# Gated cross-attention with routed experts: a hand-set list of slots in place of three-stage turns, and the last tile through all experts

## The chip, the cores and the metric

The kernel runs on one core of a Trainium2 chip. The time is the device time in microseconds, as the median of three runs; lower is better.

## The reference

For each of 8 batches of 112 tokens (256 wide) the layer attends with 16 heads of 16 over 375 context rows (192 wide), adds the gated result to x, and sends each token to one of 8 experts with room for 112 tokens each.

```python
x = x + jnp.tanh(g_xattn[0]) * _L0_xattn_ref(_layernorm(x), ctx_768, ctx_768, Wq, bq, Wk, bk, Wv, bv, Wo, bo)
x = x + jnp.tanh(g_ffn[0]) * _L0_ffn_ref(_layernorm(x), wg, W, b)
# _L0_xattn_ref:
attn = jax.nn.softmax(jnp.einsum('bhqd,bhkd->bhqk', q, k) * SCALE, axis=-1)
out = jnp.einsum('bhqk,bhkd->bhqd', attn, v)      # heads side by side, @ Wo + bo
# _L0_ffn_ref:
idx = jnp.argmax(probs, axis=-1)
locations = jnp.cumsum(mask, axis=0) - mask       # place of a token in its expert
mask = mask * (locations < C)                     # C = 896 / 8 = 112
exp_out = jnp.einsum('ech,efh->ecf', exp_in, W) + b[:, None, :]
out = jnp.einsum('tec,ecf->tf', combine, exp_out) # combine holds the gate
```

## The kernel before, in words

**Accuracy.** Scores are made in bf16 at float32 accuracy: K and Q are each split into three bf16 parts (the high part, the rest rounded, and what then remains), and six products of parts are stacked as 96 contraction rows. DMAs lay the parts of all heads into these rows (`lay_rows`, L340, K at L347, Q at L350: six of each a batch). Three more rows hold ones under K and the negated row maxima (again in three parts) under Q, so that the turned scores come out with the maximum already taken off.

**Turns.** A step t (L353 on SyncE, L518 on TensorE, L676 on ScalarE, L843 on VectorE, L1001 on GpSimd) works on three batches at once: it projects K, Q and V of batch t, takes the plain scores and their maxima of batch t-1, and the turned scores, exponentials and probability products of batch t-2. Steps 0, 1, 8 and 9 are written out, 2 to 7 are two turns of a loop of three steps (`turns`, L285). A step has 12 units; `heads_of` (L85), `AT_K1`, `AT_V2` and their like say what a unit holds.

**TensorE in a step.** K and Q of half 0 at the start (`project_kq`, L424), a second K half (L408), Q (L418) and its bias (L421) in the units, the scores (L442) into the banks `sc0` and `sc1` by turns, four turned heads a unit (L450), the product with V (L459), and at the end V (L435) and the product with Wo (L514). `scores` of a step wait for the copies of K and Q rows (L538), the first turned unit for the row of maxima (L530).

**The others.** VectorE takes each maximum from its bank (L848), subtracts the high part (`split`, L839), splits the maxima (L878 to L882), normalises the probability product (L904 to L911) and adds x (`add_x`, L820). ScalarE copies the projections out and rounds (L637), and exponentiates (L686). GpSimd makes the third part (L1007). SyncE issues the row copies.

**Router and experts.** Tiles 0 to 6 are routed together (`route`, L766, `assign`, L791), tile 7 after its own x2; GpSimd scatters all eight tiles into slots in DRAM (L962). They are cleared first (L364), read back by expert (L381), turned and multiplied (L606), and stored by an indirect DMA for each expert (L1050).

Of the kernel before, what the change touches and what calls it, by code (L numbers as in the profile page):

```python
# [26 lines left out]
QC = NK  # L53
KQ = NK + NQ
# [4 lines left out]

TWO_ONES = float(np.array([0x3F803F80], np.uint32).view(np.float32)[0])  # L60
MAXROW = 128 - 3
FAR = 4096
RING = 3

AT_K1, AT_Q1, AT_SPLIT1 = (1, 2), (3, 4), 5
FIRST_HEADS = 1
AT_V2, AT_V2E = (6, 7), 9
AT_V_OF_1 = (2, 3, 5, 6, 8, 9)
AT_MAXT, AT_MAXT_B = 11, 10

EARLY = 5
NORMED = ((0, B - 2), (B - 2, B - 1), (B - 1, B))
ROUTED = ((0, B - 1), (B - 1, B))


AT_STAT2, AT_NORM2, AT_TURN2 = 2, (5, 6, 7), (6, 7, 8)
AT_X1, AT_NORM6, AT_TURN3, AT_ROUTE, AT_PLACES = 1, 3, (2, 3, 4, 6), 8, 9
# [4 lines left out]
THREE = 4  # L82


def heads_of(unit):  # L85

    at = 2 * (unit - FIRST_HEADS)
    return range(max(at, 0), min(at + 2, H))


def build(nc, x, ctxT, gx, gf, wq, bq, wk, wv, wo, bo, wg, wT, be, out):
    slots = nc.dram_tensor("slots", (SLOTS, ROW), F32).ap()
    out_rows = out.rearrange("b n d -> (b n) d")
    with ExitStack() as stack:
# [6 lines left out]

        wq_sb = sb("wq_sb", [128, 2, D])
        bq_sb = sb("bq_sb", [1, D])
        wk_sb = sb("wk_sb", [128, 2, D])
        wv_sb = sb("wv_sb", [128, 2, D])
        wo_sb = sb("wo_sb", [128, 2, D])
        bo_sb = sb("bo_sb", [NQ, D])
        tbo = sb("tbo", [NQ, D])
        wg_sb = sb("wg_sb", [128, 2, E])
        wT_sb = sb("wT_sb", [128, E, 2, D])  # L110
        be_sb = sb("be_sb", [NQ, E, D])
# [4 lines left out]
        ones_row = sb("ones_row", [1, NQ])  # L116
# [3 lines left out]
        expert_no = sb("expert_no", [NQ, B, E])  # L120

# [3 lines left out]
        ctx_sb = sb("ctx_sb", [128, RING, 2, NK])  # L125
# [17 lines left out]

# [4 lines left out]
        onorm = sb("onorm", [128, 2, NQ])  # L148
        st2 = sb("st2", [NQ, B, 6])
# [21 lines left out]
        xin = sb("xin", [CAP, E, ROW])  # L171

        xinT, yb, res = xnT, xn, x_sb

# [7 lines left out]

        s_x = sem("first_x_loaded")
        s_xrest = sem("x_rest_loaded")
        s_gate = sem("gates_loaded")
        s_tanh = sem("tanh_ready")
# [4 lines left out]
        s_bo = sem("bo_loaded")  # L191
# [3 lines left out]
        s_pad = sem("rows_96_on_ready")  # L195
        s_vones = sem("v_ones_ready")
        s_ctx = sem("ctx_loaded")
        s_ctx1 = sem("ctx_1_loaded")
# [5 lines left out]
        s_kq = sem("kq_in_psum")  # L204
        s_hi = sem("kq_hi_ready")
        s_rest = sem("kq_rest_ready")
        s_mid = sem("kq_mid_ready")
        s_parts = sem("kq_parts_ready")
        s_lo = sem("rest_used")
        s_first = sem("first_kq_read")  # L210
        s_k6 = sem("kq_rows_laid")
        s_k60 = sem("kq_rows_of_0_laid")
# [7 lines left out]
        s_lastrows = sem("last_max_rows_ready")  # L220
        s_identv = sem("identity_for_dve")
# [3 lines left out]
        s_pv = sem("pv_in_psum")  # L225
        s_on = sem("normalised")
        s_op = sem("wo_product_in_psum")
        s_x1 = sem("x1_ready")
        s_outx = sem("x1_in_out")
        s_xn2a = sem("xn2_of_0_to_2_ready")  # L230
        s_xn2 = sem("xn2_ready")
        s_nmean = sem("first_rstd_ready")
        s_wg = sem("wg_loaded")
        s_wT = sem("experts_loaded")
# [3 lines left out]
        s_tri = sem("triangle_ready")  # L238
        s_eno = sem("expert_numbers_ready")
# [5 lines left out]
        s_empty = sem("empty_rows_ready")  # L245
# [7 lines left out]
        s_free = sem("product_read")  # L253
        s_be = sem("expert_biases_loaded")
        s_res = sem("result_ready")
        s_out = sem("out_stored")
# [3 lines left out]
        class Seen:  # L260

            def __init__(self):
                self.n, self.base = {}, {}

            def start_turn(self):
                self.base = dict(self.n)

            def __call__(self, s, more=1):  # L270
                had = self.n.get(s.name, (s, 0))[1]
                self.n[s.name] = (s, had + more)
                return had + more

        def settle(eng, seen):


            eng.drain()
            for name, (s, n) in seen.n.items():
                before_turn = seen.base.get(name, (s, 0))[1]  # L280
                if n > before_turn:
                    eng.sem_inc(s, before_turn - n)
            seen.n = {name: seen.base.get(name, (s, 0)) for name, (s, n) in seen.n.items()}

        def turns(eng, seen, step):  # L285


            for t in range(2):
                step(t, t)
            seen.start_turn()  # L290
            with eng.Fori(0, (B - 2) // RING) as i:
                for k in range(RING):
                    step(2 + k, 2 + k + RING * i)
                settle(eng, seen)
            for t in range(B, B + 2):
                step(t, t)

        def front(t):
            return t < B

# [797 lines left out]
```

## Time and profile before

| | us |
|---|---|
| median of 3 runs | 296.07 (293.12 to 302.96) |
| profiled execution | 294.2 |
| its span, first to last instruction | 292.5 |
| TensorE busy, granted clock | 200.9 (69%), 0.819 |
| VectorE busy | 139.9 (48%) |
| ScalarE busy | 87.0 (30%) |
| GpSimd busy | 63.5 (22%) |

The profile gives busy times for each engine, and for each idle stretch what ended it. Matmuls are pipelined, so that the distance from one start to the next tells more than a duration. A float32 call of the source stands as two instructions in the trace. PE is TensorE, DVE VectorE, ACT ScalarE, POOL GpSimd, SP SyncE. The granted clock is a share of 2.4 GHz.

### The profile page before, as it was taken

What the parts mean: (1) busy time and instruction counts of PE and PEld (TensorE: products, weight loads), DVE (VectorE), ACT (ScalarE), POOL (GpSimd) and SP (SyncE); (2) the same over time, 40 slices, a digit from 0 to 9 for tenths busy, and PEclk for the clock granted to TensorE, in tenths of its full rate; (3) what the DMA queues carried; (4) which work ended last, traced back from release to release, by engine and by line L of the source; (5) the groups of instructions that cost most, each with busy time, mean ns of one, the idle gap of its engine ahead of it and who ended that gap; (6) DMA issues with size and microseconds to landing.
All of it is one profiled execution on the core that took longest, in us unless ns stands there. A gap on an engine that the chain in (4) does not pass through costs nothing. (4 is left out here: it accounts for less than half of the span.)

```text
span 292.5 us, 4359 instructions
## 1 busy us (share of the span) xinstructions
PE 200.9 (69%) x1703; PEld 126.1 (43%) x1703; DVE 139.9 (48%) x311; ACT 87.0 (30%) x180; POOL 63.5 (22%) x67
## 2 busy tenths in 40 slices
PE   2685148399569975997399659957981998712590
PEld 1463024266335643554156326633640566512370
DVE  4179948248405731573167127622850764522270
ACT  1320030136122602360245125402531365400120
POOL 4439990011010101010101011001100201073064
PEclk9979558869977987699789859975995799965597
DMA  4979459806980895079409930990399948052731
GB/s 132 228 73 98 37 60 121 69 0 65 119 64 2 83 124 43 0 88 123 37 0 97 122 26 12 108 120 6 43 99 154 321 136 237 2 158 87 221 94 53
DMA packets 36840, 26.77 MB, mean 92 GB/s; under 512 B 15528, under 2 KB 34074, under 8 KB 36714
## 3 DMA queue, kind: packets, MB, share of 16 engines
q1 hardware_dynamic: 32453, 21.40, 59.7%
q10 hardware_dynamic: 3349, 2.67, 3.5%
q0 software_dynamic: 1024, 2.51, 2.8%
q8 instruction: 9, 0.15, 0.3%
q14 instruction: 5, 0.04, 0.1%
HBM read 9.25 MB, written 5.52 MB: 51 GB/s over the span
## 5 line engine op out<-in xcount | busy, mean ns | idle before, releaser
L848 DVE TENSOR_REDUCE nmax<-sc 112x1 f32<-112x375 f32 x128 | 67.2, 546 | 58.4 <-PE sc L442 57.5
L686 ACT ACTIVATE prob<-stp 128x448 f32<-128x448 f32 (+1 forms) x80 | 43.0, 542 | 69.1 <-PE stp L450 68.2
L442 PE MATMUL sc<-k,q 125*112 125x375 bf16 x128 | 45.7, 386 | 20.9 <-DMA k<-parts 15.9
L1007 POOL TENSOR_TENSOR parts<-rest,parts 128x487 bf16<-128x487 f32 x16 | 17.1, 1071 | 157.2 <-ACT parts L637 157.0
L408 PE MATMUL pj<-ctx_sb,wk_sb 128*128 128x375 f32 x64 | 35.0, 666 | 17.8 <-DMA ctx_sb<-in_ctxT 17.1
L450 PE MATMUL stp<-q,k 128*128 128x112 bf16 (+1 forms) x320 | 33.1, 238 | 14.6 <-DMA q<-mrows 14.6
L459 PE MATMUL pv<-prob,v_sb 128*32 128x112 f32 (+1 forms) x768 | 38.5, 281 | 0.4 <-ACT prob L686 0.3
L450 PEld LDWEIGHTS stp<-q,k 128*128 128x128 bf16 (+1 forms) x320 | 22.6, 124 | 27.2 <-issue 16.9
L442 PEld LDWEIGHTS sc<-k,q 125*112 125x112 bf16 x128 | 17.8, 149 | 31.6 <-DMA k<-parts 17.1
L839 DVE TENSOR_TENSOR rest<-pj,parts 128x487 f32<-128x487 f32 x16 | 10.5, 659 | 34.0 <-ACT parts L637 34.0
L459 PEld LDWEIGHTS pv<-prob,v_sb 128*32 128x32 f32 (+1 forms) x768 | 15.8, 111 | 23.7 <-issue 14.8
L408 PEld LDWEIGHTS pj<-ctx_sb,wk_sb 128*128 128x128 f32 x64 | 15.3, 257 | 23.7 <-DMA ctx_sb<-in_ctxT 13.3
L637 ACT ACTIVATE parts<-pj 128x487 bf16<-128x487 f32 x16 | 9.2, 578 | 38.3 <-PE pj L421 38.3
L435 PE MATMUL pj<-wv_sb,ctx_sb 128*128 128x256 f32 (+1 forms) x72 | 19.1, 388 | 0.0
L763 DVE TENSOR_SCALAR xn<-x_sb,mv,rs 112x256 f32<-112x256 f32 x8 | 17.1, 2182 | 3.3 <-POOL rs L957 3.3
L637 ACT ACTIVATE parts<-rest 128x487 bf16<-128x487 f32 x16 | 9.7, 608 | 19.5 <-DVE rest L839 18.9
L418 PEld LDWEIGHTS pj<-xnT,wq_sb 128*128 128x128 f32 x64 | 12.1, 225 | 4.1 <-issue 1.9
L435 PEld LDWEIGHTS pj<-wv_sb,ctx_sb 128*128 128x128 f32 (+1 forms) x72 | 12.7, 187 | 2.0 <-issue 1.0
L418 PE MATMUL pj<-xnT,wq_sb 128*128 (+1 forms) x64 | 12.1, 303 | 0.5 <-DMA bq_sb<-in_bq 0.5
L962 POOL DMA_INDIRECT slots<-rows,slot x8 | 8.0, 1006 | 13.8 <-DVE slot L804 12.1
L435 PE MATMUL stp<-wv_sb,ctx_sb 128*128 128x256 f32 (+1 forms) x24 | 9.0, 511 | 2.1 <-DMA wv_sb<-in_wv 2.1
L1050 POOL DMA_INDIRECT out<-x_sb,xin x8 | 7.8, 972 | 12.2 <-issue 12.2
(100 smaller groups left out, 200.7 us busy)
## 6 DMA issues: line engine op xcount, KB each, us to landing
k<-parts SPq DMA_DIRECT2D x48, 187.5 KB, 7.3
q<-parts SPq DMA_DIRECT2D x48, 56.0 KB, 6.9
ctx_sb<-in_ctxT SPq DMA_DIRECT2D x8, 281.2 KB, 7.2
wT_sb<-in_wT ACTq DMA_DIRECT2D x1, 2048.0 KB, 14.7
slots<-xin SPq DMA_DIRECT2D x1, 1799.0 KB, 15.8
xin<-slots SPq DMA_DIRECT2D x8, 224.9 KB, 5.0
be_sb<-in_be SPq DMA_DIRECT2D x1, 896.0 KB, 6.1
x_sb<-in_x SPq DMA_DIRECT2D x1, 784.0 KB, 11.6
```

The costliest lines, as they stand in the source:

```text
L408: pe.matmul(pj[m][:, 0:NK], wk_sb[:, c, m * 128:(m + 1) * 128], ctx_sb[:, t % RING, c, :], start=(c == 0), stop=(c == 1))
L418: pe.matmul(pj[m][:, QC:KQ], wq_sb[:, c, cols], xnT[:, bass.ds(tb, 1), c, :], start=(c == 0), stop=False)
L435: mm = pe.matmul(bank[0:kn, at:at + D], ctx_sb[:, t % RING, c, k0:k0 + kn], wv_sb[:, c, :], start=(c == 0), stop=(c == 1))
L442: pe.matmul(sc[h % 2][0:NQ, 0:NK], q6[0:MAXROW, b3, h, :], k6[0:MAXROW, b3, h, :], start=True, stop=True).then_inc(s_sc, 1)
L450: mm = pe.matmul(bank_of_sT(t, n)[0:kn, j * NQ:(j + 1) * NQ], k6[:, b3, h, k0:k0 + kn], q6[:, b3, h, :], start=True, stop=True)
L459: mm = pe.matmul(pv[32 * j:32 * j + 32, g * NQ:(g + 1) * NQ], v_sb[0:kn, b3, c, 4 * g + j, :], prob[0:kn, n % 3, j * NQ:(j + 1) * NQ], sta ...
L637: nc.scalar.activation(dst, src, ACT.Copy).then_inc(signal, 1)
L686: nc.scalar.activation(prob[0:kn, n % 3, :], bank_of_sT(t, n)[0:kn, 0:4 * NQ], ACT.Exp, scale=SCALE).then_inc(s_p, 1)
L763: nc.vector.tensor_scalar(xn[:, b, :], x_sb[:, b, :], mv1[:, b, 0:1], rs1[:, b:b + 1], ALU.subtract, ALU.mult).then_inc(s_xn, 1)
L839: nc.vector.tensor_tensor(rest[:, m, :], pj[m][:, 0:KQ], parts[:, t % RING, 0, m, :], ALU.subtract)\
L848: nc.vector.tensor_reduce(nmax[:, h:h + 1], sc[h % 2][0:NQ, 0:NK], axis=AX.X, op=ALU.max, negate=True).then_inc(s_max, 1)
L1007: ins = nc.gpsimd.tensor_tensor(parts[:, t % RING, 2, m, :], rest[:, m, :], parts[:, t % RING, 1, m, :], ALU.subtract)
```

## The change

1. **Slots.** All engines run through one list of slots from -4 to 120, twelve a batch, without a loop. At slot s, `at(s, offset)` tells which batch and which of its twelve places stands there. A batch's scores begin at 12b, its K projection at 12b-16, its K rows are laid at 12b-7, V is projected at 12b+12 to 12b+17 (batch 0: 2 to 7), the maxima are split at 12b+13 and turned at 12b+14, turned scores begin at 12b+17, products with V a slot later, the normalisation stands at 12b+30, Wo at 12b+31, x is added at 12b+32, and the logits come at 12b+36.
2. **Q** is made for groups of 1, 4 and 3 batches, all early, and laid by 18 DMAs in place of 48. Its bias is added as ScalarE copies it out and VectorE subtracts.
3. **K's split**: ScalarE copies the projection out twice (bf16 and float32, `k_hi`, `k_copy`), and from batch 1 on GpSimd does both subtractions and the rounding (`k_split`). K's rows of a partition lie side by side, so that a copy has half as many pieces of twice the length (1500 bytes). GpSimd also splits the maxima.
4. **Context** stays whole in SBUF, loaded in four DMAs; there is no ring. The score product has 96 rows in place of 125 and needs no zeros there.
5. **Router.** Tiles 0 to 5 are routed at slots 97 to 99, tile 6 at 109 to 111, and both are scattered while attention of batch 7 still runs.
6. **Last tile.** Tile 7 is not scattered. It is multiplied by all eight experts (`dense`, 8 calls of 512 columns), and VectorE adds the eight products with a weight which is the token's gate for its expert and 0 elsewhere. The biases come by a product of the turned weights with the expert biases.

Cut to its core (the code after):

```python
HEADS = ((0, 1), (2,), (3,), (4, 5), (6,), (7,), (8, 9), (10,), (11,), (12, 13), (14,), (15,))
K_AT, KE_AT, KSPLIT_AT, LAY_AT = -16, (-14, -12), (-13, -11), -7
V01_AT, V01E_AT, V2_AT, V2E_AT, V_EARLY = 12, 16, 16, 18, -10
SPLITMAX_AT, MAXT_AT, MROW_AT, T_AT, PV_AT = 13, 14, 15, 17, 18
NORM_AT, WO_AT, ADD_AT, LN_AT, X2T_AT, LG_AT = 30, 31, 32, 33, 35, 36
QG = ((0, 1), (1, 5), (5, 8))
...
# TensorE
for s in range(FIRST, LAST + 1):
    if s == 0: turn_xn(1); project_q(1, 0); project_q(1, 1)
    if (found := at(s, T_AT)): scores_T(*found)
    if (found := at(s, S_AT)): scores(found[0], HEADS[found[1]][0])
    if (found := at(s, K_AT, 4)) and found[0] > 0: project_k(*found)
    ...
    if s == 5: turn_xn(2)
    if s in (6, 7): project_q(2, s - 6)
    ...
    if found := at(s, PV_AT): probs_v(*found)
pe.wait_ge(s_wT, 16 * E)
dense(0); dense(1); places(2, *R2); dense(2); dense(3)
...
# SyncE
def lay_k(b):
    if b >= KR: sp.wait_ge(s_st, UNITS * (b - KR + 1))
    for part, ready in ((0, s_khi), (1, s_kmid), (2, s_klo)):
        sp.wait_ge(ready, 2 * (b + 1))
        ...
# GpSimd
def k_split(b, m):
    ...
    nc.gpsimd.tensor_tensor(kf[:, b % 2, m, :], kf[:, b % 2, m, :],
                            parts_k[:, b % 2, 0, m, :], ALU.subtract).then_inc(s_krest, 1)
    pool.wait_ge(s_krest, 2 * b + m + 1)
    nc.gpsimd.tensor_copy(parts_k[:, b % 2, 1, m, :], kf[:, b % 2, m, :]).then_inc(s_kmid, 1)
    k_lo(b, m)
for s in range(FIRST, LAST + 1):
    if s == 2: q_lo(1, 0); q_lo(1, 1)
    if s == 4: rstd(2)
    if found := at(s, SPLITMAX_AT, 1): split_max(found[0])
    for m in range(2):
        if (found := at(s, KSPLIT_AT[m], 1)) and found[0] > 0: k_split(found[0], m)
    if s == 6: constants()
    if s == 9: q_lo(2, 0); q_lo(2, 1)
    ...
# VectorE, of the slots that the text speaks of
    if s == 2: statistics(5, 8)
    if s == 4: normalise(2)
# VectorE, after the slots
for e in range(E):
    link(nc.vector.scalar_tensor_tensor(last[:, :], banks[e // 2][0:NQ, (e % 2) * D:(e % 2 + 1) * D],
         share[:, e:e + 1], src, ALU.mult, ALU.add))
```

On TensorE, at the seam of two steps of the loop, before (stp is a bank of turned scores, sc one of scores, pj one of a projection, mparts the parts of the maxima):

```order
L558 MATMUL sc<-ident_b,mparts 48x112
L459 MATMUL pv<-prob,v_sb 32x112 x8
L435 MATMUL pj<-wv_sb,ctx_sb 128x256 x4
L514 MATMUL misc<-wo_sb,onorm 112x256 x2
L408 MATMUL pj<-ctx_sb,wk_sb 128x375 x2
L418 ISA
L418 MATMUL pj<-xnT,wq_sb 128x112
L418 ISA
L418 MATMUL pj<-xnT,wq_sb 128x112
L421 MATMUL pj<-ones_row,bq_sb 128x112
L450 MATMUL stp<-q,k 128x112 x8
L442 MATMUL sc<-k,q 112x375
```

And the slots 6 to 8 of a later batch now, where a batch's last product with V has just passed (L425 scores, L438 turned scores, L456 product with V, L478 Wo, L400 K):

```order
L425 MATMUL sc<-k,q 112x375 x2
L456 MATMUL pv<-prob,v_sb 32x112 x4
L438 MATMUL stp<-q,k 119x112 x4
L425 MATMUL sc<-k,q 112x375
L478 MATMUL misc<-wo_sb,onorm 112x256 x2
L456 MATMUL pv<-prob,v_sb 32x112 x4
L438 MATMUL stp<-q,k 128x112 x4
L425 MATMUL sc<-k,q 112x375
L400 MATMUL pj<-ctx_sb,wk_sb 128x375
L456 MATMUL pv<-prob,v_sb 32x112 x4
L438 MATMUL stp<-q,k 128x112 x4
L425 MATMUL sc<-k,q 112x375
```

V, Wo, K and Q stood together between two batches' turned scores, and there was no score among them; now Wo stands between a score and a product with V of the next batch, and K is spread over slots.

On SyncE's queue, in a step of the loop before (parts copied into the k and q rows, and the load of a context):

```order
L350 DMA q<-parts 16x16x112 x2
L355 ISA
L355 DMA ctx_sb<-in_ctxT 96x2x375
L350 DMA q<-parts 16x16x112
L347 DMA k<-parts 16x16x375 x2
L350 DMA q<-parts 16x16x112 x2
L347 DMA k<-parts 16x16x375 x2
L350 DMA q<-parts 16x16x112
```

Now, for a batch in the middle (L334 the row of maxima, L312 six K copies, L317 two experts' weights, whose tile shares its room with x's turned rows under the name early):

```order
L334 DMA q<-mrows 3x16x112
L312 DMA k<-parts_k 16x8x750 x6
L317 DMA early<-in_wT 128x512 x2
L334 DMA q<-mrows 3x16x112
L312 DMA k<-parts_k 16x8x750 x6
```

The Q copies and the context loads have gone from the steady part, and the row of maxima, which ScalarE's queue issued before, stands ahead of the next K copies.

On GpSimd, the end of its constants and what follows, before (L1020 adds the bias to x, L1007 is the third part):

```order
L997 IOTA expert_no 112x64
L1020 TENSOR_TENSOR x_sb<-x_sb,tbo 112x2048
L1007 TENSOR_TENSOR parts<-rest,parts 128x487 x2
L291 UNCONDITIONAL_BRANCH
L1007 TENSOR_TENSOR parts<-rest,parts 128x487 x6
```

At slot 9 GpSimd's stream has Q's last group (L977), x plus bias (L1051) and seven constants; this is the end of the constants and what follows them, up to the first half of batch 2's K and the first maxima (L967, L970 and L961 are a half's subtraction, rounding and subtraction; L985 to L988 split the first maxima):

```order
L1024 MEMSET every 112x112
L1025 MEMSET before 112x112
L1026 AFFINE_SELECT before<-before 112x112
L1029 IOTA expert_no 112x64
L967 TENSOR_TENSOR kf<-kf,parts_k 128x375
L970 CAST parts_k<-kf 128x375
L961 TENSOR_TENSOR parts_k<-kf,parts_k 128x375
L985 CAST mparts<-nmax 112x16
L986 TENSOR_TENSOR mrest<-nmax,mparts 112x16
L987 CAST mparts<-mrest 112x16
L988 TENSOR_TENSOR mparts<-mrest,mparts 112x16
```

The first maxima are behind the last Q group, the bias, the constants and one half of K's split.

## Rows read from the trace of the kernel before

**Rows 1.** The page, its part 1: busy us (share of the span), instructions
```profile
PE 200.9 (69%) x1703; PEld 126.1 (43%) x1703; DVE 139.9 (48%) x311; ACT 87.0 (30%) x180; POOL 63.5 (22%) x67
```

**Rows 2.** Table by stretch: from:to, length, engines busy (instructions), granted clock, DMA share, GB/s
```profile
0.00:41.00 41.00, 18.84 (x68) 12.25 (x68) 24.87 (x32) 8.89 (x17) 27.91 (x29) 0.82 0.68 103
91.00:101.00 10.00, 10.00 (x126) 6.07 (x124) 8.09 (x17) 6.04 (x12) 1.05 (x1) 1.00 0.44 49
102.45:131.40 28.95, 23.55 (x198) 14.22 (x199) 12.96 (x28) 9.60 (x19) 2.22 (x2) 0.82 0.62 63
241.10:254.70 13.60, 11.43 (x179) 8.19 (x179) 5.72 (x24) 7.22 (x17) 0.81 (x2) 1.00 0.46 129
254.70:292.50 37.80, 14.43 (x66) 10.86 (x66) 12.42 (x39) 3.43 (x10) 16.65 (x18) 0.68 0.40 119
```

**Rows 3.** List of waits: who <- whom, us in total, times, longest us
```profile
...
DVE nmax L848 <- PE sc L442: 57.5, 63, 7.9
...
PE sc L442 <- DMA k<-parts: 15.9, 6, 4.7
...
PE stp L450 <- DMA q<-mrows: 14.6, 6, 5.7
...
```

**Rows 4.** Timeline of TensorE, 84 to 101.5: start us, us, engine, line, operation
```profile
90.94 0.79 PE L408 MATMUL pj<-ctx_sb,wk_sb 128*128 128x375 f32 x2
91.57 0.32 PE L442 MATMUL sc<-k,q 125*112 125x375 bf16 x1
...
92.15 0.37 PE L450 MATMUL stp<-q,k 128*128 128x112 bf16 x4
92.36 0.33 PE L442 MATMUL sc<-k,q 125*112 125x375 bf16 x1
92.52 0.37 PE L418 MATMUL pj<-xnT,wq_sb 128*128 x2
...
92.98 0.40 PE L459 MATMUL pv<-prob,v_sb 119*32 119x112 f32 x8
93.32 0.37 PE L450 MATMUL stp<-q,k 128*128 128x112 bf16 x4
...
96.65 0.60 PE L435 MATMUL pj<-wv_sb,ctx_sb 128*119 128x256 f32 x2
97.08 0.32 PE L442 MATMUL sc<-k,q 125*112 125x375 bf16 x1
```

**Rows 5.** Costliest groups of the page; then the timeline of VectorE after a batch
```profile
L848 DVE TENSOR_REDUCE nmax<-sc 112x1 f32<-112x375 f32 x128 | 67.2, 546 | 58.4 <-PE sc L442 57.5
...
102.45 0.65 DVE L904 STREAM_TRANSPOSE pvT<-pv 128x448 f32<-128x448 f32 x1 [0.88 <-PE pv L459]
...
103.84 0.41 DVE L911 STREAM_TRANSPOSE onorm<-onT 128x224 f32<-128x224 f32 x1
```

**Rows 6.** Timeline, 237 to 262: the last row of maxima, its copy and use
```profile
239.91 0.26 ACT L637 ACTIVATE mrows<-sc 48x112 bf16<-48x112 f32 x1 [0.21 <-PE sc L558]
...
242.56 0.57 PE L450 MATMUL stp<-q,k 128*128 128x112 bf16 x8 [1.52 <-DMA q<-mrows]
```

**Rows 7.** Timeline of the lead-in; a costly group and a DMA group of the page
```profile
22.55 13.98 DVE L763 TENSOR_SCALAR xn<-x_sb,mv,rs 112x256 f32<-112x256 f32 x5 [1.66 <-POOL rs L957]
22.65 7.96 POOL L982 MEMSET k<- 32x3000 f32 x3
...
L1007 POOL TENSOR_TENSOR parts<-rest,parts 128x487 bf16<-128x487 f32 x16 | 17.1, 1071 | 157.2 <-ACT parts L637 157.0
...
k<-parts SPq DMA_DIRECT2D x48, 187.5 KB, 7.3
```

**Rows 8.** Timeline of GpSimd at the end: the first and the last of eight stores
```profile
278.66 0.94 POOL L1050 DMA_INDIRECT out<-x_sb,xin  x1 [9.52 <-issue]
...
288.15 0.94 POOL L1050 DMA_INDIRECT out<-x_sb,xin  x1 [0.30 <-issue]
```

More of the change, by code:

```diff
@@ L52 @@
 UNITS = G * NCH
-QC = NK
-KQ = NK + NQ
 K_PART = (0, 0, 0, 1, 1, 2)
@@ L257, in build @@
+        s_last = sem("last_tile_ready")
         s_chain = sem("vector_chain")
         s_pchain = sem("gpsimd_chain")
[L260 to L299, printed above, removed]
-        def maxima(t):
-            return 1 <= t <= B
-        def attention(t):
-            return t >= 2
@@ new lines, in _ @@
+            pe.wait_ge(s_wT, 16 * E)
+            dense(0)
+            dense(1)
+            places(2, *R2)
+            dense(2)
+            dense(3)
+            pe.wait_ge(s_share, 1)
+            pe.transpose(sc[0][0:E, 0:NQ], share[:, :], ident[0:NQ, 0:NQ]).then_inc(s_shareT, 1)
+            pe.wait_ge(s_shareTe, 1)
+            pe.wait_ge(s_be8, 16)
+            pe.matmul(pv[0:NQ, 0:D], shareT[:, :], be8[:, :], start=True, stop=True).then_inc(s_bias, 1)
+            for e in range(E):
+                turn_xin(e)
+                if e == 1:
+                    pe.wait_ge(s_last, 1)
@@ new lines, in _ @@
+            for e in range(E):
+                if e % 2 == 0:
+                    dve.wait_ge(s_dense, e // 2 + 1)
+                src = rows[:, b, X1:X1 + D] if e == 0 else last[:, :]
+                link(nc.vector.scalar_tensor_tensor(
+                    last[:, :], banks[e // 2][0:NQ, (e % 2) * D:(e % 2 + 1) * D], share[:, e:e + 1],
+                    src, ALU.mult, ALU.add))
+            dve.wait_ge(s_bias, 1)
+            nc.vector.tensor_tensor(last[:, :], pv[0:NQ, 0:D], last[:, :], ALU.add).then_inc(s_last, 1)
@@ L960, in scatter, with rstd @@
-            def scatter(lo, hi):
-                for b in range(lo, hi):
-                    nc.gpsimd.indirect_dma_start(
-                        slots, bass.IndirectOffsetOnAxis(ap=slot[:, b:b + 1], axis=0), rows[:, b, :],
-                        None, bounds_check=SLOTS - 1, oob_is_err=False).then_inc(s_scat, 16)
+            link = Chain(pool, s_pchain)
+            def rstd(g):
+                lo, hi = QG[g]
+                pool.wait_ge(s_stat, g + 1)
+                link(nc.gpsimd.tensor_scalar(ve1[:, lo:hi], mv1[:, lo:hi, 1], EPS, None, ALU.add))
+                nc.gpsimd.tensor_tensor(rs1[:, lo:hi], ve1[:, lo:hi], half[:, lo:hi], ALU.pow)\
+                    .then_inc(s_rstd, 1)
@@ L966, in _, with scatter @@
+            def scatter(b):
+                nc.gpsimd.indirect_dma_start(
+                    slots, bass.IndirectOffsetOnAxis(ap=slot[:, b:b + 1], axis=0), rows[:, b, :],
+                    None, bounds_check=SLOTS - 1, oob_is_err=False).then_inc(s_scat, 16)
             link(nc.gpsimd.memset(ident[:, :], 0.0))
@@ L1033, in step @@
[L1033 to L1045 removed]
+                    more_constants()
```

1252 lines of the change are left out of this document (672 added, 580 removed).

## The prediction

> **What bounds the kernel now.** I read four views in this order. The page's busy times come first: TensorE 69%, VectorE 48% of a 292.5 us span [rows 1]. No engine is full, so the time lies in waits between them. The table by stretch shows where [rows 2]. The first 41.0 us hold no score at all, only loads, projections and splits. Then comes a turn of the loop per batch: 102.45 to 131.40 is one, 28.95 us long, from one batch's finished probability product to the next, and it holds only 12.96 us of VectorE, 9.60 of ScalarE and 2.22 of GpSimd work. Inside it 23.55 us of TensorE are called busy, but at a mean clock of 0.82. The drain after the last loop turn (241.10 to 254.70) takes 13.60 us at full clock, and the tail after it 37.80 us.
>
> Who is waited for inside a turn? The list of waits names two DMAs, each six times: the k rows for the scores, 15.9 us in all and 4.7 at the longest, and the rows of maxima for the turned scores, 14.6 [rows 3]. Both stand at the seam of two turns: TensorE ends a batch, projects, waits for maxima and for rows which were only just split, and only then scores. Between the seams it does its work densely: 10.00 us busy in 91 to 101, clock 1.00, in which 8.09 us of VectorE lie beside it [rows 2]. So a turn is some 15 us of dense work and some 13 us of seam.
>
> **The change, part by part.** The turn disappears. In a list of slots, 12 a batch, each slot has one turned unit, one or two scores, at most one projection call and one probability product. K of a batch is projected 16 slots ahead of its first score, its rows are laid from slot -7 or earlier, and turned scores come 17 slots after the scores begin, no longer 24 units. Four terms follow.
>
> *A batch in steady state.* I take TensorE's costs from start to start at clock 1.00 [rows 4]. Turned unit: 92.15 to 92.36, 0.21; a third of them have the 119-wide chunk, for which I take 0.27; 12 of them 2.8. Score: 92.36 to 92.52, 0.16, by 16 is 2.6. K call: 90.94 to 91.57, 0.63, by 4 is 2.5. V call: 96.65 to 97.08, 0.43, by 6 is 2.6. Probability product: 92.98 to 93.32, 0.34, by 12 is 4.1. The product with Wo is two calls of a V call's width, 0.9. The turns of maxima and of x2 and the logits are not in these rows; I set 0.8 for them, between 0.3 (bare columns) and 1.5. Sum 16.3 us. VectorE has 16 maxima of 0.546 [rows 5] = 8.7, then 1.8 for the normalisation (102.45 to 104.25, [rows 5]) and about 1.2 for adding x and its statistics: 11.7, so it is cover and not bound on the mean. It is bound at one place. In slot 6 the normalisation stands ahead of two maxima. TensorE has there only 1.1 us of work, then score 10 waits for maximum 8, which is done 0.2 + 1.8 + 0.55 = 2.6 us after the product ended. That costs 1.5. A second place is the row of maxima: it is turned late in slot 2 and read at slot 5, with 2.6 to 2.8 us of TensorE work between. Before, the rows left ScalarE at 240.17 and TensorE took them up at 242.56, 2.4 us [rows 6]; with 0.5 for the turn and the copy it is 2.9, so 0.2 is late. Batch: 16.3 + 1.5 + 0.2 = 18.0; I take 18.2. Bounds are 16.3 (every stall hidden) and 28.95 (nothing won).
>
> [...]
>
> *What moves to GpSimd.* From batch 1 on, both subtractions and the rounding between them are its own. A subtraction took 1.071 us for 487 columns [rows 7], so 0.82 for 375; the rounding has no row, and lies between 0.34 (a memset by the column, 7.96 us for 9000, [rows 7]) and 0.82, I take 0.6, nearer the subtraction since it too reads and writes SBUF. Two halves: 4.5 us; the split of the maxima about 1.3, variance and normalisation of x2 1.5: 7.3 of 18.2. The cover is slot 11 to slot 3. If it were gone, the maxima row is late next. The k copies are 6 DMAs of 187.5 KB. From batch 3 on they wait until the turned scores of three batches back are done, 8 slots or 12 us ahead of their use. Now such a copy lands 7.3 us after its issue (median, [rows 7]); six issues one after the other add some 3 us. That is 10.3 of 12, just hidden, and q's copies are no more among them.
>
> *Lead-in.* Slot 17, the first turned unit, is the mark. Statistics of four tiles, their normalisations (each waits for a GpSimd op), the turns and q projection of 448 columns on a TensorE at lower clock, and q's split on three engines put the first maximum at about 27 us, where the present one comes after 41 [rows 2]. Then normalisations of tiles 5 to 7 meet GpSimd's constants. The trace shows what that costs: five took 13.98 us from 22.55, as GpSimd wrote its memsets [rows 7], 2.8 each and each ending with a memset. Three cost 8 here, and end at 40 after 7 maxima (3.8) and statistics (1.9). Turn and q projection of the last group take till 45, its splits till 47.5, then GpSimd's queue stands in front of the first maxima: 4.5 for x plus bias (2048 columns at the subtraction's 2.2 ns), 2 for constants, 2.3 for one half of a k split, 1.3 for the maxima: 58. Three more for the row: slot 17 starts at 61. TensorE waits in slot 14 for it. Bounds: 50 (these collisions absent) and 70.
>
> *Slots 17 to 95* are 79 slots, 6.58 batches: 119.8, less 2.5 for four K calls that slots 80 to 83 have no more: 117.3. *Slots 96 to 113*: twelve as in the present drain, 13.6 [rows 2], and six with a V call at 1.0, and 1.4 for waits on the mask: 21.0. *Tail.* Now it is 24.0 us to the first indirect store at 278.66, eight of them about 1.25 to 1.4 apart, and 3.4 us after the last ends at 289.09 [rows 8]. The last tile's scatter and reload go, and the variance no longer stands behind five scatters. Added are 8 calls of 512 columns, 0.86 each by the K call = 6.9, and eight multiply-adds which lie beside them but for the last two, then shares, bias and add 2.0. About 8 from the last product to the logits, 6.9 + 0.8 for the dense products, 3.5 for what follows and 1.5 to the first store: 20.7. So the tail is 34.5; eight stores a queue apart end it whichever product comes first. Half clock there would add 7.
>
> Sum: 61 + 117.3 + 21.0 + 34.5 = 233.8 us of span, against 292.5. The profiled execution took 294.2, 1.7 over its span, so 235.5; it lies 1.9 under the median 296.07. I forecast **236 us**.
>
> **The rivals.** *The ping-pong holds*: two banks of scores and one VectorE queue make each slot wait for a maximum. For it speaks that 57.5 us of VectorE's idle time end with a score, the longest 7.9 [rows 3], so the two engines do hand over all the time; against it, that 8.09 of 10.00 us of VectorE were busy in the dense stretch [rows 2], more than the 11.7 of 18.2 that it now has. Some 3.3 us more a batch, 21.5: 141.5 - 2.5, so 258. *The stalls hide*: slots 6 and 7 absorb more, maxima arrive early, lead-in 55: 16.4 a batch, 105.4 + 55 + 21 + 33 + 1.7 = 216. *Slower*: the dense stream is not granted its full clock. The present kernel had 1.00 for 13.6 us at a time [rows 2], with rests between, never for 120. At the lower of the two levels (1.2 and 2.4 GHz) 16.3 us becomes 32.6 a batch, 215 for slots 17 to 95, 31 for the drain and 7 more in the tail: 61 + 212 + 31 + 41.5 + 1.7 = 347. It decides for slower from 28 a batch, that is when the clock's mean falls under 0.6. Against it is that both dense stretches of [rows 2] show 1.00, and that the lower means belong to stretches with waits. *The change does not overlap*: a K copy that must wait for the turned unit of three batches back, then lands late: with 20 us of landing a batch takes 26, 287 us in all. Its place is the first score of batches 3 to 7. Against it: the DMA rings are shared by fewer transfers, since q's 48 copies become 18.
>
> **How the numbers follow.** My forecast holds for 226 to 247: 0.50. Ping-pong, 247 to 270: 0.22. Hidden stalls, under 226: 0.17. No overlap, 270 to 302: 0.07. Slower by the clock: 0.04. Low and high, 213 to 264, leave out 2 in 10. A measurement of this kernel tells about 2% from no change: under 290 is faster, 0.93; 290 to 302, 0.03; over it 0.04.
>
> **What would show it.** Slot periods of 1.5 us between turned units 12 to 95, clock above 0.95 there; score 10 of each batch waiting about 1.5 us for a maximum; no wait over 1 us for k rows; normalisations of tiles 5 to 7 of 2.7 us each; first turned unit near 61 us; first indirect store 21 us after the last product. Wrong it would be with k rows among the longest waits in steady state, with GpSimd's split over 10 us a batch, or with a clock that stays under 0.8.

## The result and the profile after

| | before | changed |
|---|---|---|
| median, us | 298.8 (4 runs, 293.12 to 302.96) | 262.09 (4 runs, 261.26 to 274.37) |
| profiled execution; span | 294.2; 292.5 | 262.34; 260.6 |
| mean granted clock | 0.819 | 0.805 |

The ratio is 0.8887 (95% interval 0.8773 to 0.9001): 11% faster, and 26 us slower than the 236 that I forecast; the time lies at the upper end of the range. Ratios here compare only the executions of each kernel that lie within 1.5% of its fastest, and medians take in all of them. First the page of the changed kernel, its busy times and two of the lines with 40 slices of 6.5 us each (a digit is tenths):

```profile
PE 209.8 (80%) x1656; PEld 121.5 (47%) x1656; DVE 131.4 (50%) x289; ACT 89.1 (34%) x200; POOL 93.6 (36%) x145
...
PE   1865771961599999998998989987999999659890
...
PEclk9997755695555555999999999999555999957997
```

Against [rows 1] TensorE goes from 69% to 80% busy. The second line to read is PEclk: seven slices of 5 in a row from the tenth on and three in a row later, most of them under slices of PE that are full. (Three more fives stand in the lead-in and the tail, among waits.) At half clock a matmul takes twice as long, so a busy TensorE there is a slow one. The table by stretch cuts the span at my forecast's marks (first turned unit, slot 96, the end of the last product with V), and adds one batch in steady state and the stretches at half clock (columns as in [rows 2]):

```profile
0.00:68.15 68.15, 37.44 (x100) 21.43 (x101) 34.50 (x58) 15.42 (x35) 37.19 (x50) 0.76 0.99 144
68.15:205.60 137.45, 131.63 (x1219) 75.96 (x1219) 72.22 (x147) 58.66 (x128) 39.10 (x72) 0.79 0.56 90
205.60:224.96 19.36, 17.98 (x257) 11.16 (x252) 8.13 (x40) 11.23 (x26) 8.53 (x13) 1.00 0.26 79
224.96:260.60 35.64, 22.72 (x85) 12.98 (x85) 16.55 (x46) 3.74 (x12) 8.76 (x11) 0.82 0.29 81
...
117.61:135.88 18.27, 17.30 (x194) 10.40 (x193) 11.23 (x23) 9.46 (x21) 7.25 (x13) 1.00 0.64 95
...
68.15:104.00 35.85, 35.72 (x224) 18.96 (x224) 14.07 (x28) 11.22 (x23) 6.08 (x13) 0.50 0.69 111
...
183.00:203.00 20.00, 19.88 (x140) 11.45 (x139) 8.72 (x19) 5.55 (x12) 0.80 (x2) 0.50 0.19 59
```

A batch at full clock takes 18.27 us where a turn took 28.95 [rows 2], and I had said 18.2. But in the 35.85 us behind the first turned unit, and in 20 us more from 183, TensorE is 99% busy at a clock of 0.50. Slots 17 to 95 took 137.45 us, not 117.3.

What stood before each fall of the clock? The timeline of TensorE (in brackets the idle time before, and what ended it):

```profile
63.58 0.26 PE L469 MATMUL misc<-ident_b,mparts 112*48 112x112 bf16 x1 [6.31 <-POOL mparts L988]
...
68.15 0.56 PE L438 MATMUL stp<-q,k 99*128 99x112 bf16 x4 [2.62 <-DMA q<-mrows]
...
138.16 0.37 PE L425 MATMUL sc<-k,q 96*112 96x375 bf16 x1 [0.77 <-DVE nmax L774]
...
182.16 0.37 PE L425 MATMUL sc<-k,q 96*112 96x375 bf16 x1 [1.60 <-DMA k<-parts_k]
```

The first fall of the two (just before 60) is in the 6.3 us for which TensorE waits for GpSimd's split of the first maxima. The second (about 183) follows the wait of the last batch's first score for its k rows. The wait of 0.77 at 138.16, one such in each batch, is the one behind the normalisation, and no fall follows it. Against [rows 3], the two DMA waits at the seams, 15.9 and 14.6 us in all, are down to 2.1 and 2.6.

### The profile page after: what moved, and what is told of

It reads as the page before. It is cut to its first block, busy times and chain, and to the rows that moved or that the text cites. A ratio compares the mean times of both kernels' runs of the same rounds, so it can differ in the third digit from the quotient of the medians.

```text
span 260.6 us, 4263 instructions
## 1 busy us (share of the span) xinstructions
PE 209.8 (80%) x1656; PEld 121.5 (47%) x1656; DVE 131.4 (50%) x289; ACT 89.1 (34%) x200; POOL 93.6 (36%) x145
## 4 chain that ended last, share of the span: by engine, by line
PE 63%; DVE 15%; POOL 7%; DMA 6%; issue 3%; ACT 2%; SPq 1%; POOLq 0%; DVEq 0%
PE pv L456 12%; PE stp L438 11%; PE pj L411 9%; PE sc L425 8%; PE pj L400 7%; DVE early L754 5%; PE stp L381 3%; PE misc L478 3%; DMA k<-parts_k 3%; PE pj L516 2%; DVE nmax L774 2%; POOL out L1071 2%; DVE pvT L781 2%; POOL x_sb L1051 2%; DMA x_sb<-in_x 2%
## 5 line engine op out<-in xcount | busy, mean ns | idle before, releaser
L425 PE MATMUL sc<-k,q 96*112 96x375 bf16 x128 | 48.6, 395 | 8.5 <-DVE nmax L774 5.8
L438 PE MATMUL stp<-q,k 99*128 99x112 bf16 (+1 forms) x384 | 42.3, 241 | 2.6 <-DMA q<-mrows 2.6
L456 PE MATMUL pv<-prob,v_sb 128*32 128x112 f32 (+1 forms) x768 | 43.0, 300 | 1.6 <-issue 1.3
L438 PEld LDWEIGHTS stp<-q,k 99*128 99x128 bf16 (+1 forms) x384 | 26.5, 122 | 22.9 <-issue 19.9
L411 PE MATMUL pj<-wv_sb,ctx_sb 96*128 96x256 f32 (+3 forms) x96 | 36.5, 469 | 0.0
L400 PE MATMUL pj<-ctx_sb,wk_sb 96*128 96x375 f32 (+1 forms) x64 | 31.4, 593 | 5.7 <-DMA ctx_sb<-in_ctx 5.7
L456 PEld LDWEIGHTS pv<-prob,v_sb 128*32 128x32 f32 (+1 forms) x768 | 16.3, 116 | 34.7 <-issue 20.7
L425 PEld LDWEIGHTS sc<-k,q 96*112 96x112 bf16 x128 | 19.1, 156 | 17.0 <-DVE nmax L774 11.1
L411 PEld LDWEIGHTS pj<-wv_sb,ctx_sb 96*128 96x128 f32 (+3 forms) x96 | 21.1, 235 | 0.5 <-issue 0.4
L967 POOL TENSOR_TENSOR kf<-kf,parts_k 128x375 f32<-128x375 f32 x14 | 12.6, 899 | 23.2 <-ACT kf L623 23.2
L400 PEld LDWEIGHTS pj<-ctx_sb,wk_sb 96*128 96x128 f32 (+1 forms) x64 | 14.3, 239 | 8.4 <-issue 7.8
L961 POOL TENSOR_TENSOR parts_k<-kf,parts_k 128x375 bf16<-128x375 f32 x16 | 13.5, 847 | 5.4 <-ACT parts_k L623 4.3
L754 DVE TENSOR_SCALAR early<-x_sb,mv,rs 112x256 f32<-112x256 f32 x8 | 13.9, 1785 | 2.6 <-POOL rs L945 2.6
L478 PE MATMUL misc<-wo_sb,onorm 128*112 128x256 f32 x32 | 10.9, 474 | 2.3 <-DVE onorm L791 2.3
L977 POOL TENSOR_TENSOR parts_q<-early,parts_q 128x112 bf16<-128x112 f32 (+2 forms) x6 | 4.4, 749 | 14.6 <-ACT parts_q L623 14.6
```

Source lines behind the costliest of these rows:

```text
L400: mm = pe.matmul(pj[m][:, 0:NK], wk_sb[0:rows_in, c, m * 128:(m + 1) * 128], ctx_sb[0:rows_in, b, c, :], start=(c == 0), stop=(c == 1))
L411: mm = pe.matmul(pj[n // 2][0:kn, (n % 2) * D:(n % 2 + 1) * D], ctx_sb[0:rows_in, b, c, k0:k0 + kn], wv_sb[0:rows_in, c, :], start=(c == 0 ...
L425: pe.matmul(sc[h % 2][0:NQ, 0:NK], q6[0:PROD, h, q_cols(b)], k6[0:PROD, b % KR, h, :], start=True, stop=True).then_inc(s_sc, 1)
L438: mm = pe.matmul(stp[n % 2][0:kn, j * NQ:(j + 1) * NQ], k6[0:MAXROWS, b % KR, h, k0:k0 + kn], q6[0:MAXROWS, h, q_cols(b)], start=True, sto ...
L456: mm = pe.matmul(pv[32 * j:32 * j + 32, g * NQ:(g + 1) * NQ], v_sb[0:kn, b % VR, c, 4 * g + j, :], prob[0:kn, n % 3, j * NQ:(j + 1) * NQ], ...
L478: mm = pe.matmul(misc[0:NQ, 0:D], onorm[:, g, :], wo_sb[:, g, :], start=(g == 0), stop=(g == 1))
```

## Experiments

Dummy products are matmuls into a bank that is free at that time; nothing reads what they write. The kernel before, run beside the experiments, had medians of 295.2 to 297.3. Two of its 36 executions there took 845.8 us at a clock of 1.00, and no trace of them says why.

**Does the wait take the clock?** The first kernel fills the wait:

```diff
+                        warm(pv, 9)          # ahead of turn_max(0)
+                    warm(pv, 5)              # ahead of scores_T(0, 0)
+ # warm: n times pe.matmul(bank[:, 0:NK], wk_sb[0:KC, 0, 0:128], ctx_sb[0:KC, 0, 0, :])
```

> Fourteen dummy products (375 columns, f32, into the bank of the weighted sums, which is free then) are given to TensorE before the turn of the maxima (9) and before the first turned unit (5), where it waited 6.3 and 2.6 us. They are no part of the computation. Theory A (the clock falls because TensorE waits there, and the mixed stream behind it does not bring it back for 36 us): the granted clock stays at 1.00 from 57 us through 118, the batch behind the first turned unit takes 18.3 to 20 us instead of 29.0, and the time falls by 11 to 15 us, to 247 to 251. Theory B (the rival: a stream as dense as this one is not granted the full clock for long, whatever came before): the clock falls to 0.50 all the same within the first batch, and the time stays at 260 to 266.

Measured: 250.08 us (248.3 to 250.21), ratio 0.8484 (0.842 to 0.8549). The windows of this run:

```profile
56.00:118.00 62.00, 58.76 (x572) 34.23 (x571) 32.84 (x67) 26.84 (x59) 27.60 (x54) 1.00 0.81 129
168.00:187.00 19.00, 18.88 (x128) 10.78 (x126) 8.06 (x17) 5.22 (x12) 0.00 (x0) 0.50 0.16 51
```

The clock is 1.00 through 118 and on to 166, and four executions lie within 2 us. Added work made the kernel 12 us faster. Theory B falls: the dense stream of slots 17 to 83 is granted the full clock. The second fall, at 167, is still there, behind a wait of 1.58 for k rows.

Then all places at once: these fourteen, three ahead of the last batch's first score (`if s == 84: warm(pj[0], 3)`), and eight of 512 columns in the tail.

> The changed kernel with its own order of transfers and GpSimd, and dummy products only where TensorE waits: the fourteen of the first run, three ahead of the first score of the last batch, eight of 512 columns in the last tile's tail. Theory A: from the first run's 250.1, the batch behind slot 84 takes 17 to 18.5 us instead of 23.9 and the tail's stretch at half clock goes (2 to 3 us): 240 to 243, mean clock above 0.92, all six executions within 3 us. Rival: the clock falls near slot 84 whatever is put there; 248 to 251.

```profile
0.00:67.80 67.80, 43.61 (x128) 25.44 (x129) 34.63 (x58) 15.44 (x35) 37.26 (x50) 0.85 0.99 145
67.80:183.60 115.80, 109.50 (x1227) 65.12 (x1225) 72.09 (x147) 58.76 (x128) 39.17 (x72) 1.00 0.67 107
...
183.60:204.77 21.17, 18.77 (x257) 11.55 (x253) 7.96 (x40) 11.15 (x26) 8.49 (x13) 0.95 0.24 73
204.77:241.20 36.43, 28.36 (x101) 15.35 (x101) 16.55 (x46) 3.75 (x12) 8.84 (x11) 0.87 0.28 79
```

Median 243.79, ratio 0.826 (0.8199 to 0.8321), five of six executions at 242.4 to 244.6. Slots 17 to 95, which took 137.45, take 115.80 us at clock 1.00, with the same instructions in the same order and three dummies more. Filling the wait kept the clock at both places. How sure is it that the unfilled wait took it? At the first place it fell in all eight profiles without dummies there, between 57.0 and 60.5. At the second, all ten profiles without dummies there (the changed kernel's two, and those of eight experiments) have the same wait of 1.6 for k rows. In nine the clock fell within 2 us of its end, but in one (the memsets moved, below) it stayed at 1.00:

```profile
184.03 0.37 PE L426 MATMUL sc<-k,q 96*112 96x375 bf16 x1 [1.58 <-DMA k<-parts_k]
```

That profile fell only at 217. In the five profiles with dummies there the clock never fell at that place. So a wait of 1.6 us in this stream nearly always costs the clock, not always, and what decides is not shown. The tail gained nothing (36.43 against 35.64): its clock rose from 0.82 to 0.87, and its dummies added as much as that gave; in this run the clock was at half once more from about 203 to 210. One of the six executions was granted 0.551 on the mean and took 334.62, and three kernels below have one execution each at 0.70 to 0.72 (292 to 295 us). None of these four was profiled, so where their clock was low is open.

**Does it hang on the clock from run to run?** The changed kernel itself, six times more:

> The changed kernel itself, six executions more. Theory A: every execution's time goes by the clock it was granted: from the runs so far (251.9 us at 0.871, 262 at 0.81, 276.9 at 0.747, 293.6 at 0.697 over several variants) each 0.01 of mean clock is worth about 2.3 us, and the executions lie at 255 to 280 with clocks 0.74 to 0.84. Rival (the spread comes from transfers or from the chip's other work): times differ by more than 5 us at clocks that agree within 0.01.

Measured: 265.06 (264.12 to 277.23). With the four of the result there are ten executions: 261.3 to 265.9 us at clocks of 0.789 to 0.81, 274.37 at 0.757 and 277.23 at 0.748. From 264.12 at 0.800 to 277.23 at 0.748 that is 2.5 us for each 0.01, and where clocks agree within 0.01 the times agree within 3.3 us; the rival wanted over 5. The window 68 to 104 of its profile shows the same stretch once more, 35.88 of 36 us busy at half clock:

```profile
68.00:104.00 36.00, 35.88 (x235) 19.15 (x235) 14.07 (x28) 11.23 (x23) 6.37 (x13) 0.51 0.67 110
```

**What brings the clock back?** Six dummy products in slot 20, in the middle of the slow stretch, then twelve (`if s == 20: warm(misc, 6)`).

> Six dummy products (375 columns, f32) stand in slot 20, in the middle of the stretch at half clock, into the bank that the turned maxima have left: 7.5 us at half clock, 3.8 at full. They are no part of the computation. Theory C (the clock stays low because the mix of short products with weight loads between them is too thin, and a solid stream brings it back): the clock is 1.00 from about 80 us on instead of 104, the 24 us at half clock become about 13, and the time is 262 minus 11 plus 6, about 257 (254 to 259). Rival (it comes back by itself after a time, whatever runs): the clock comes back at 104 or later, and the time is 266 to 270.

```profile
74.00:76.00 2.00, 2.00 (x5) 1.13 (x4) 0.00 (x0) 0.00 (x0) 0.00 (x0) 0.50 1.11 123
76.00:78.00 2.00, 2.00 (x5) 1.01 (x5) 0.00 (x0) 0.00 (x0) 0.00 (x0) 0.61 1.03 348
78.00:94.00 16.00, 15.81 (x170) 8.81 (x169) 7.74 (x15) 7.96 (x17) 5.22 (x10) 1.00 0.37 93
...
74.45 5.49 PE L540 MATMUL misc<-ctx_sb,wk_sb 96*128 96x375 f32 x12
```

> As the run with six dummy products in slot 20, but twelve, 15 us at half clock. In the profile of six the clock was back 2.3 us after the first of them, but two of its four runs had a mean clock of 0.79. Theory C: with twelve all four runs get the clock back; each run costs 7.6 us of dummies (at full clock) and gives back 11 to 12, so all lie at 253 to 262 with mean clocks above 0.84. Rival (the return is chance and has nothing to do with the dummies): the runs spread from 255 to 275 again, and the profile shows the return at another place.

With six, the profiled execution has the clock back some 3 us after the burst begins at 74.45, where the changed kernel had it back at 104. The median was 261.87 (251.94 and 256.41 at clocks of 0.871 and 0.847; 267.34 and 268.45 at 0.788 and 0.791). With twelve it was 258.38, three executions at 257.8 to 258.6 and one at 273.22 with 0.789; in the profile the clock came back some 2 us after the burst's start at 73.47. So both profiles agree with theory C, that the burst brings it back. But 2 of 4 and 1 of 4 executions stayed low on the mean, and whether the burst failed in them or the clock fell elsewhere no profile shows. Nor is it so that the mix of short products never wins the clock back. In these two profiles it was low for some 17 us. Two kernels further down run the same stream behind a fall at 80.8 with no dummies in it, and one had the clock back at 97.9, after 17 us, the other at 128.6, after 48. Ten of these us in each are a wait, so that under 8 us of the stream were enough in the one and 38 were needed in the other. From 98 on, the late one first:

```profile
98.00:128.00 30.00, 29.88 (x190) 17.06 (x183) 11.11 (x23) 9.58 (x21) 7.32 (x13) 0.50 0.25 31
...
98.00:243.00 145.00, 133.91 (x1360) 79.61 (x1357) 83.58 (x206) 63.07 (x143) 50.80 (x85) 1.00 0.45 85
```

A return by chance after 17 us is therefore not excluded for the burst in slot 20, though behind the fall before slot 17 no profile without dummies had one in under 37 us. Theory C is likely and not shown.

**Who sets the first turned unit?** My sum put GpSimd's queue there. This kernel moves the bias and the constants behind the split of the first maxima:

```diff
                     for m in range(2):
                         q_lo(2, m)
+                if s == 14:
                     pool.wait_ge(s_tbo, 1)
                     pool.wait_ge(s_xn, B)
```

(Q's last group, `q_lo(2, m)`, stays in slot 9; the two waits and the bias and constants behind them now belong to slot 14.)

> GpSimd adds the bias to x and writes the router's constants in slot 14, behind the split of the first maxima, instead of slot 9 ahead of it; nothing else changes. Both theories: the wait for the split (6.3 us) goes to under 1.5, the maxima row lands near 62 to 64 instead of 68.15. Theory A: with less idle time the clock may stay up; then the time is 242 to 250. Theory B: only the 4 to 6 us of the wait are gained: 256 to 258.

The split was done at 56.13 instead of 63.44, and the first turned unit came only 0.5 earlier. The queue of transfers and TensorE:

```profile
57.00 0.87 SPq L334 DMA_DIRECT2D q<-mrows  x1
...
67.63 0.55 PE L438 MATMUL stp<-q,k 99*128 99x112 bf16 x4 [9.54 <-DMA q<-mrows]
```

The waits of 6.3 and 2.6 us became one of 9.5: the row, issued at 57.00, stood behind 1.0 MB of q rows and 0.84 MB of context. All seven profiles with this order of transfers reach slot 17 at 67.3 to 68.6, this one too, whose split ends at least 6 us before the others'. The time was 269.88 (255.31 to 276.87), clocks 0.747 to 0.833.

A kernel that keeps this edit, moves the memsets to GpSimd's first slot and puts only the context load later (slot 18) missed its aim:

> As the run before, and the memsets under the keys and V go into GpSimd's first slot (about 23 us, while it and VectorE wait for the q projection), and the load of context tiles 5 to 7 moves from slot 8 to slot 18. The normalisations of tiles 5 to 7, 8.0 us beside the memsets, should take 1 to 3 us, the first maximum stay near 31, and the first turned unit come near 57 to 60 instead of 68.15. Theory A: clock 1.00 behind it, time 238 to 246. Theory B: 250 to 254. If the transfers (busy 1.1 in every window from 46 to 80) are the bound behind the memsets, the first turned unit stays at 62 to 64 and the gain over the run before is under 2 us.

```profile
18.73 9.73 DVE L755 TENSOR_SCALAR early<-x_sb,mv,rs 112x256 f32<-112x256 f32 x4 [1.49 <-POOL rs L946]
...
43.41 1.05 DVE L755 TENSOR_SCALAR early<-x_sb,mv,rs 112x256 f32<-112x256 f32 x3
...
18.82 7.96 POOL L1015 MEMSET k<- 3x3000 f32 x3
```

Without memsets beside them the three normalisations of tiles 5 to 7 take 1.05 us, not 7.99; but now the four of tiles 1 to 4 stand beside them, 9.73 instead of 3.36. That shifts what follows by some 7 us (the first maximum comes at 38.26), and the k rows of batch 1 then end a wait of 9.4. First turned unit at 71.15, 263.66 us (259.01 to 293.55). For the first turned unit the collision on an earlier link was worse than where it was. This is the kernel whose profiled clock stayed up at the second place, and two executions at 259.0 and 259.4 lie under all of the changed kernel's in spite of the later slot 17; that the clock is the reason I infer.

The transfers themselves, in the order of need, with GpSimd's move kept:

```diff
-                if s == 8:
-                    lay_q(2)
-                    load_ctx(3, 5, 8)
+                if s == 18:
+                    lay_q(2)
+                    load_ctx(3, 5, 8)
```

> GpSimd's bias and constants in slot 14 as in the second run, and on the transfer queue the q rows of tiles 5 to 7 (first used in slot 60) and the load of context tiles 5 to 7 (first used in slot 44) go from slot 8 to slot 18, behind the first row of maxima and the k rows of the third batch. Theory D (the first turned unit waits for the queue of transfers, 1.0 MB of q rows and 0.84 MB of context ahead of a row of 10.5 KB): the row issued near 57 lands near 60 and the first turned unit stands at 60 to 62 instead of 67.6 to 68.2. Rival (the queue of GpSimd alone set it, as I predicted): it stands at 67 as in the second run. The time goes with the clock that is granted behind it: 253 to 257 at a mean of 0.81, 243 to 246 if it stays full.

```profile
57.35 0.86 SPq L334 DMA_DIRECT2D q<-mrows  x1
...
59.62 0.56 PE L440 MATMUL stp<-q,k 99*128 99x112 bf16 x4 [1.28 <-DMA q<-mrows]
```

First turned unit at 59.62: theory D holds. Moving the transfers alone was not run. By an estimate it would have given under 2 us of the 8.5: the split ends at 63.44 in the changed kernel, and here the first turned unit stands 2.9 behind the split's end at 56.68, which makes 66.4 instead of 68.15. So the two queues hid each other. The time was 255.24 (254.69 to 255.89), 0.8655 (0.8588 to 0.8722), 7 and 10 under the two medians of the changed kernel, at a clock that is a little higher (0.818 against 0.80 to 0.81); at 2.5 us for 0.01 some 3 to 5 of that are the clock's. The clock fell here too, at 59, after idle gaps of only 0.2 to 0.6 us and in one of 1.3; between them stood single scores, 2.16 us of work in the 4 from 56 to 60. So no long wait was needed there: in the changed kernel, too, the stretch ahead of the long wait was thin (2.19 us of work in the 4 from 54 to 58), and the 6.3 us alone are not shown to be what took the clock.

Six more kernels go on from this order, five of them with dummies. In most the clock fell at the next weak place.

> As the run before, with four dummy products (375 columns, f32, no part of the computation) ahead of the first turned unit. Theories A and D together: first turned unit at 60 to 62, clock 1.00 from there through the sixth batch, time 250.1 less 6 to 7 us, 243 to 245. If theory A is wrong about what holds the clock (the 28 dummy passes of the first run and not the absence of a wait), the clock falls within the first batch and the time is 253 to 258.

> As the run before, and three dummy products ahead of the first score of the last batch (where TensorE waits 1.6 us for k rows and the clock then stays at 0.50 for 20 us), and eight solid ones of 512 columns between the small products of the last tile's tail. Theory A: the batch behind slot 84 takes 17 us instead of 23.9, the tail's stretch at 0.50 (17 us) goes, mean clock 0.95 or more, time 233 (230 to 238). Rival (the second fall has another cause, such as the length of the stretch at full clock): the clock falls near slot 84 all the same, and the time is 242 to 246.

Medians 268.83 (249.2 to 295.26) and 248.61 (246.96 to 248.8). The clock fell at 60 while the four dummies in slot 17 ran, and was back at 64, where the kernel with the same order and no dummies had it back at 96. At 80 it fell again, in a wait of 11.5 us for the second row of maxima, behind the pile that now stood in slots 18 to 20:

```profile
90.36 0.56 PE L440 MATMUL stp<-q,k 99*128 99x112 bf16 x4 [11.50 <-DMA q<-mrows]
```

Up to slot 84 these two kernels are the same, and they are the two that had the clock back after 48 and after 17 us. From 98 on, with slot 84 filled, the second kernel kept 1.00 up to 243.

> GpSimd's bias and constants in slot 14; the load of context tiles 5 to 7 in slot 30, the q rows of tiles 5 to 7 in slot 43, and the eight fills of the token buffer (1.8 MB) two at a time in slots 33, 45, 57 and 69 instead of all in slot 20. No dummies. Theory D: first turned unit at 59 to 61, and the second row of maxima, which waited 1.9 and 11.5 us behind this pile in the runs before, lands without a wait over 1 us. With the clock at half behind slot 17 as before, 252 to 256; if it stays full, 240 to 245.

> As the run before, with dummy products (375 columns, f32): two in slot 12, three in slot 14, two in slot 17, three before the first score of the last batch, and eight of 512 columns in the last tile's tail. They are no part of the computation. Theories A and D: first turned unit at 61 to 62, clock 1.00 from 48 us to the end of the products, no wait of TensorE over 2 us between slots 17 and 96, time 61.5 + 117.3 + 19 + 33 + 1.8 = 233 (230 to 238). If the clock falls near 60 as it did with four dummies in slot 17 alone, 244 to 250.

> As the run before, and in the lead-in: the memsets under the keys for the first two batches behind the normalisations of tiles 1 to 4 instead of beside those of tiles 5 to 7, the third in slot 14, and six dummy products where TensorE waits for the normalisations (18 to 22 us). The normalisations of tiles 5 to 7 take 1.1 us instead of 8.0 (as in the third run), the q projection 2.8 to 3.5 instead of 5.6, and the first turned unit comes at 55 to 58; time 3 to 5 us under the run before, 228 to 230. Rival: the memsets hold the second rest of q (28 to 33 us) in their place, and it is the same within 1.5 us.

Medians 265.03 (255.52 to 267.74), 258.34 (254.87 to 260.77) and 248.75 (three at 248.6 to 248.8, one 292.04). All three medians missed their numbers. The first had its first turned unit at 59.20 and no late row of maxima behind it, as expected, but half clock from 58 until 126 in the profiled execution, 68 us with TensorE 98% busy; one execution, at 0.826, took 255.52, inside the range. The second held 1.00 up to 70, then lost it at a wait of 1.57 for k rows, and again at 126 in one of 4.70 for a row of maxima: q rows, weights and fills were issued within one batch, and the DMA share was 1.10 in that wait. In the third the normalisations of tiles 5 to 7 did go down to 1.05, but TensorE then waited 8.9 us for the k rows of batch 1, and 4.4 at 121. I read the transfers as the bound there, and the next kernel doses them by batch, with two dummies more in slot 24:

> New order of transfers: context tiles 5 to 7 in slot 18, one third of their q rows' copies in slot 31 and two thirds in slot 43, the eight fills of the token buffer in slots 20 (two), 57 and 69 (three each), so that each batch has 13.5 to 16.5 us of transfers in 18.3; GpSimd's bias and constants in slot 14; dummies as in the run of the name spread_warm and two more in slot 24. Theory D: no wait over 1.5 us for a row of maxima between slots 17 and 96, first turned unit at 61, clock 1.00 from 48 on, time 233 to 238. If rows still come 4 us late once, the clock falls behind that wait and the time is 244 to 252.

```profile
0.00:62.88 62.88, 41.49 (x115) 24.03 (x115) 34.41 (x58) 15.42 (x35) 34.05 (x43) 0.78 0.82 121
62.88:180.70 117.82, 110.97 (x1230) 65.93 (x1231) 72.09 (x147) 58.70 (x128) 42.25 (x80) 1.00 0.80 124
180.70:201.59 20.89, 18.53 (x257) 11.34 (x253) 7.92 (x40) 11.10 (x26) 8.25 (x13) 0.97 0.24 74
201.59:238.30 36.71, 28.67 (x101) 15.48 (x101) 16.56 (x46) 3.74 (x12) 9.04 (x11) 0.87 0.28 79
```

Median 238.91 (238.59 to 240.06), ratio 0.8096 (0.8035 to 0.8157): the best version, 19% under the kernel before and some 23 us under the changed one. No wait in slots 17 to 95 is over 0.8 us. It differs from the second of the three in the order of transfers and in those two dummies; how much of the 19.4 us between them each gave, no run separates. Its stretches lie beside my terms: 62.88 for 61, 117.82 for 117.3, 20.89 for 21.0, 36.71 for 34.5.

## Why the prediction was right and wrong

| term, us | forecast | changed kernel | all dummies | dosed transfers |
|---|---|---|---|---|
| first turned unit | 61 | 68.15 | 67.80 | 62.88 |
| slots 17 to 95 | 117.3 | 137.45 | 115.80 | 117.82 |
| slots 96 to the last product | 21.0 | 19.36 | 21.17 | 20.89 |
| tail | 34.5 | 35.64 | 36.43 | 36.71 |
| span | 233.8 | 260.60 | 241.20 | 238.30 |

The miss of 26.8 is 7.2 + 20.1 - 1.6 + 1.1.

*A batch in steady state: right, 18.27 for 18.2*, with errors that cancel, and that is luck. TensorE's content was 17.30, not 16.3. The stall of score 10 was 0.77, not 1.5, and the row of maxima was never late in a steady batch, where I had 0.2. Ping-pong and hidden stalls are out as rivals at full clock. (The sum of the ping-pong rival comes to 257, not 258.)

*GpSimd: right*, 7.25 us a batch for 7.3. *The k copies "just hidden": nearly.* They landed in 6.7 (median) and were late for batch 1, by 0.52, and for the last batch, by 1.60, and for none between. The forecast took 2.5 off for the K calls that slots 80 to 83 no longer have; it did not ask what these calls had covered.

*The step that failed: "clock above 0.95 there".* It carries 20 of the 26.8 us. I priced every term from slot 17 on at clock 1.00 and set against it one rival, "the dense stream is not granted its full clock", with a place (slots 17 to 95) and all or nothing in time: 347 us at 0.04. The waits that I had in the sum myself ("TensorE waits in slot 14 for it") were charged with their own length only. The runs show that such a place, a wait and the thin work around it, can also cost the clock behind it, here 36 and 20 us of stream at half speed, and that the stream does not win it back at once by being busy. Filled with dummies at both places, the same stream takes 115.80 us at 1.00, so the dense stream itself is not refused. Why one profile kept the clock through the second wait, and what ends a stretch at half clock (10 to 68 us long, behind falls between slots 12 and 84), stays open. The Trainium skill, "TensorE: Matmul & The Clock Gate", section "What's actually happening", says that the default state is throttled and activity releases the throttle. Here 35.72 busy us of 35.85 passed before it was released; the measurement decides, and TensorE's busy share in the profile does not tell when the clock comes back.

*The lead-in: the mark was missed by 7.2, and its step too.* The first maximum came at 31.27, not 27; the q projection ran mostly at half clock (5.61 us), which explains at most 2.8 of the 4.3. The collision with the memsets was right, 7.99 for 8. GpSimd's queue ended at 63.44, not 58, and the row took 4.7 from there, not 3. But "then GpSimd's queue stands in front of the first maxima" named only one of two bounds. From 46 to 80 the DMA share was 1.09 on the mean, and the row waited for the queue of transfers. I had counted transfers (q's 48 copies become 18) and not bytes ahead of the row.

*Drain and tail: right within 1.6 and 1.1.* The first indirect store came 22.6 us after the last product for 20.7; a stretch at half clock, 227 to 237, lies between.

## What to carry to other kernels

Charge a wait of TensorE with more than its length: read the granted clock behind each wait, and how long it stays down. Where it stays down, a few products into a free bank inside the wait gave 12 us here for one place and 18 to 21 for all, in most executions and not in all. When an edit makes TensorE's stream denser, add up the bytes that each batch puts on the queue of transfers, and which small late row stands behind them. Two bounds that end together hide each other: taking one away and seeing no gain does not clear it.

## What the runs showed of the hardware

- TensorE 99% busy for 36 and for 20 us stayed at 0.50, and 98% busy for 68 us in one profile. Behind the same fall the same stream had 1.00 back after 17 us in one profile and after 48 in another. Bursts of f32 products of 375 columns were followed by it within 2 to 5 us in four profiles.
- Waits of 1.6 us in the dense stream were followed by a fall in nine profiles of ten, and the waits of 0.77 behind the normalisation by none.
- The same program was granted means of 0.748 to 0.81 in ten executions, and its time went with it, 2.5 us for 0.01.
- Normalisations of 256 columns on VectorE take 0.35 us each alone (1.05 for three) and 2.7 each beside GpSimd's memsets, each as long as one memset (7.97 for three).
- On one queue a row of 10.5 KB took 10.6 us from its issue to its use behind 1.8 MB, and 2.3 without that ahead of it.
